# In the selective scan, VectorE runs both channel tiles' scans of a unit before the column copies and the products with C

## The reference, cut to what matters

```
xs = silu(conv(in_proj(x)))                          # 512 channels
dt = softplus(dt_proj(x_dbl[..., :16]) + dt_proj_b)
Bv, C = x_dbl[..., 16:32], x_dbl[..., 32:48]         # 16 states
a = exp(dt[..., None] * A)                           # A = -exp(A_log)
u = dt[..., None] * Bv[:, :, None, :] * xs[..., None]
h[t] = a[t] * h[t-1] + u[t]                          # along time, for each channel and state
y = einsum('btis,bts->bti', h, C) + xs * D_skip
```

## Time and profile before

| what | value |
|---|---|
| median of the runs | 2456.8 us (2453.07 to 2459.64) |
| the profiled execution, first to last instruction | 2453.7 us |
| PE busy | 2211.1 us (90%) |
| DVE busy | 1888.8 us (77%) |
| ACT busy | 1647.0 us (67%) |
| POOL busy | 1373.5 us (56%) |
| DMA | 430.22 MB, mean 175 GB/s |
| granted TensorE clock, mean | 0.957 |

### The profile page before, as it was taken

The page is one execution under the profiler, slowest core; times in us unless marked ns, Lnnn a source line. Parts: engine busy times, 40 slices in busy tenths (PEclk is TensorE's granted clock), DMA queues, the critical chain, the costliest instruction groups (busy, mean ns, idle before and its releaser), DMA issues.

```text
span 2453.7 us, 36941 instructions
## 1 busy us (share of the span) xinstructions
PE 2211.1 (90%) x12464; PEld 1794.1 (73%) x12464; DVE 1888.8 (77%) x3049; ACT 1647.0 (67%) x2715; POOL 1373.5 (56%) x809
## 2 busy tenths in 40 slices
PE   6788887999999996998799999999999999899986
PEld 4778776798888895887566767666676676676765
DVE  5686654566666662676898998989989899899995
ACT  6755542455555552666778787887788877878774
POOL 0103333011111115221888988989889988899895
PEclk8899988999999997999799999999999999999988
DMA  8434334566666653533465656655556566565562
GB/s 285 83 50 102 89 95 125 189 230 230 230 229 231 230 209 103 177 112 115 159 212 183 195 172 198 210 183 186 189 175 216 181 193 201 184 202 169 186 206 99
DMA packets 235434, 430.22 MB, mean 175 GB/s; under 512 B 35089, under 2 KB 117457, under 8 KB 235234
## 3 DMA queue, kind: packets, MB, share of 16 engines
q1 hardware_dynamic: 229090, 410.87, 52.3%
q0 software_dynamic: 6144, 16.79, 2.2%
HBM read 353.61 MB, written 73.96 MB: 174 GB/s over the span
## 4 chain that ended last, share of the span: by engine, by line
PE 51%; DVE 16%; issue 12%; ACT 9%; POOL 5%; DMA 4%; SPq 1%; another core or an unknown queue 1%; POOLq 1%; DVEq 0%; ACTq 0%
PE pb L1643 11%; PE pb L1616 11%; DVE pb L2096 6%; PE pb L2408 4%; PE pb L2413 4%; PE pb L996 3%; PE pb L2434 2%; PE pb L2307 2%; DVE UU L2102 2%; POOL UU L2021 2%; PE pb L2323 2%; DMA XB<-xnd 2%; PE pb L2332 2%; POOL UU L2029 1%; ACT L2233 1%
## 5 line engine op out<-in xcount | busy, mean ns | idle before, releaser
L2021 POOL TENSOR_TENSOR UU<-dx,BB 128x1024 f32<-128x1024 f32 x256 | 616.5, 2417 | 108.5 <-DMA BB<-bcd 83.7
L2233 ACT ACTIVATE pb<-dt,al 128x512 f32<-128x512 f32 x512 | 339.5, 686 | 147.9 <-DVE UU L2102 146.5
L2102 DVE TENSOR_TENSOR UU<-pb,CC 128x512 f32<-128x512 f32 x512 | 351.4, 686 | 22.4 <-DMA CC<-bcd 4.8
L2096 DVE TENSOR_TENSOR_SCAN pb<-pb,hs,UU 128x512 f32<-128x512 f32 x256 | 328.5, 1283 | 12.2 <-ACT pb L2233 8.0
L2096 DVE TENSOR_TENSOR_SCAN pb<-pb,UU 128x512 f32<-128x512 f32 x256 | 312.9, 1222 | 7.8 <-ACT pb L2233 6.4
L1533 DVE TENSOR_TENSOR HL<-HF,HH 128x512 fp32r<-128x512 f32 x220 | 159.7, 728 | 206.6 <-ACT HH L1438 198.9
L1433 ACT ACTIVATE HF<-pb,BU 128x512 f32<-128x512 f32 x192 | 132.1, 688 | 245.9 <-PE pb L1616 195.9
L1383 POOL TENSOR_TENSOR clo_b<-craw_b,chi_b 128x1024 fp32r<-128x1024 f32 x22 | 62.3, 2830 | 409.9 <-ACT chi_b L1446 409.9
L2408 PE MATMUL pb<-HAh,WH 128*128 128x512 f32 x1024 | 279.3, 415 | 8.2 <-DVE dt L2077 6.3
L1643 PE MATMUL pb<-W2h,HH 128*128 128x256 f32 x880 | 256.6, 292 | 6.3 <-issue 5.0
L2413 PE MATMUL pb<-HAl,WH 128*128 128x512 f32 x1024 | 258.2, 394 | 0.0
(11 more groups left out here) (333 smaller groups left out, 4880.3 us busy)
## 6 DMA issues: line engine op xcount, KB each, us to landing
WH<-fhd SPq DMA_DIRECT2D x176, 512.0 KB, 3.5
BB<-bcd SPq DMA_DIRECT2D x256, 256.0 KB, 4.7
CC<-bcd SPq DMA_DIRECT2D x256, 256.0 KB, 5.0
raw<-in_w1a SPq DMA_DIRECT2D x23, 1024.0 KB, 7.2
raw<-in_w2a SPq DMA_DIRECT2D x23, 1024.0 KB, 7.7
craw_b<-in_fch SPq DMA_DIRECT2D x22, 512.0 KB, 6.3
fhd<-chi_b SPq DMA_DIRECT2D x22, 512.0 KB, 3.9
fld<-clo_b SPq DMA_DIRECT2D x22, 512.0 KB, 5.1
```

The costliest lines, as they stand in the source:

```text
L2021: e.tensor_tensor(ubuf(n)[:], dx[p][:], BB[n % 3][:].rearrange("p (a m) -> p a m", a=1).to_broadcast([P, 2, 512]), ALU.mult).then_inc(p_u. ...
L2096: e.tensor_tensor_scan(h_[:], h_[:], uu[:, c, :], first, ALU.mult, ALU.add).then_inc(v_sc.sem, 1)
L2102: e.tensor_tensor(uu[:, c, :], abank(n, c)[:], CC[n % 3][:], ALU.mult).then_inc(v_mu.sem, 1)
L2233: e.activation(abank(n, c)[:], dt[p][:, c, :], ACT.Exp, scale=al1[:, 2 * p + c, s:s + 1]).then_inc(c_a.sem, 1)
```

## The change

In step `u` of VectorE's loop, the order of a unit was scan 0, copy 0, product 0, scan 1, copy 1, product 1. It becomes scan 0, scan 1, copy 0, product 0, copy 1, product 1. Copies exist in even blocks only. The wait for `CC` moves from behind scan 0 to behind scan 1. The waits for the finished scan of each tile (`v_sc`) stay in front of its copy and product. The number of instructions and their tiles are unchanged, as are the counts that the other engines wait for: `v_sc` still counts tile 0 before tile 1, and so do `c_hs` and `v_mu`.

```diff
@@ -2094,11 +2094,11 @@
                         else:
                             first = 0.0
                         e.tensor_tensor_scan(h_[:], h_[:], uu[:, c, :], first, ALU.mult, ALU.add).then_inc(v_sc.sem, 1)
-                        if c == 0:
-                            e.wait_ge(s_cl[n % 3], 16 * (n // 3 + 1))
+                    e.wait_ge(s_cl[n % 3], 16 * (n // 3 + 1))
+                    for c in range(2):
                         e.wait_ge(*v_sc.at((p, s, c), blk))
                         if blk % 2 == 0:
-                            e.tensor_copy(hs[:, 2 * i + c:2 * i + c + 1], h_[:, 511:512]).then_inc(c_hs.sem, 1)
+                            e.tensor_copy(hs[:, 2 * i + c:2 * i + c + 1], abank(n, c)[:, 511:512]).then_inc(c_hs.sem, 1)
                         e.tensor_tensor(uu[:, c, :], abank(n, c)[:], CC[n % 3][:], ALU.mult).then_inc(v_mu.sem, 1)
```

## The result

The changed kernel took 2486.3 us, the median of four runs (2484.6 to 2487.9), against 2455.5 us before: a ratio of 1.0123, interval 1.0108 to 1.0138. It is 31 us slower, more than the forecast of 2460 us and beyond the range, which ended at 2482 us. In a second comparison, beside other runs of both kernels, the ratio was 1.0113 (1.0088 to 1.0138). The profiled execution spans 2482.6 us.

The account below looks back on a forecast made before the run. The prediction saw no single engine as the bound, but a chain hopping between engines in strict order, with PE the floor. Its terms, -19 + 15 + 8 + 0 = +4 us, gave 2460 us, range 2434 to 2482.

Parts of the forecast that it names:

- Step 1: DVE's scans back to back: a unit falls from 3.92 to about 3.6 us, worth -19 us for scans on the path.
- rival (c): On DVE, a scan behind a scan does not overlap, so only the costs remain: 2480 us, chance 0.06.
- Step 2: Tile 0's product comes 0.97 us later; 15 handovers through ACT to PE, at units 14 and 25, cost +15 us.
- Step 3: ACT's other work W behind the waiting exponential stops DVE above 2.8 us, before 4.4; longer stops cost +8 us.
- Step 4: DVE's wait for CC moves behind scan 1; most of its 13.7 us disappears, counted as 0 us.
- (b): Tile 0's bank decides, where ACT's exponential waits with a table load behind it: +19 us, 2476 us, chance 0.30.
- unit pace: Sign on DVE: a unit without stops takes 3.6 us instead of 3.92.
- ACT's wait above 146.5 us: Sign on ACT: its wait for products to free a bank stays near or above 146.5 us.
- its mark of 50 us: Sign on DVE: idle time before scans with ACT as releaser rises from 14.5 us to 50 or more.

Follow-up runs that it names:

- the four-bank pair: Kernel before and changed kernel, each with four PSUM banks for the scans instead of three: 0.9984 and 0.9968 against the kernel before.
- the twelve units: Kernel before with the new order only in 12 units a block where tile 1's exponential started 0.9 us or more after product 0: 1.0001.
- the 17 units: Kernel before with the new order in the 12 units a block where no exponential waits, and in 6, 16, 17, 20 and 24: 0.9969.
- The units with long W: Kernel before with the new order in 13 units a block, nearly all with 3.9 us or more of ACT's work behind the waiting exponential: 1.0090.
- six places: Kernel before with the new order in units 6, 14, 16, 17, 20 and 24, with 1.7 us or less of ACT's work behind the exponential: 0.9960.
- four of 32: Changed kernel with the old order in units 25, 27, 29 and 31 of each block: 0.9995 against the kernel before.

## Why the prediction was wrong, step by step

**Step 1, DVE's pace**, was right in its size and wrong in its worth. Scan behind scan runs at 1.13 us (two in 2.35 us, the copy 2.26 us behind the first at 1646.99 in the trace of after), and a unit takes 3.6 us. But the term of -19 us for scans on the path was a wrong use of the chain. The chain's share says where the last result passed, and not that the rest would keep up. With the handovers gone, in the four-bank pair, the gain was some 5 us; in the twelve units there was none.

The rule of the Trainium skill's "VectorE: DVE Perf Modes", section "The DRAIN you can't avoid", that led to rival (c) does not hold here in its plain form. A scan that depends on nothing before it starts 1.13 us after one that lasts 1.2. The same section adds that a next operation that is not held starts earlier, and this the trace bears out.

**Step 2, the handover at units 14 and 25**, forecast +15 us from ACT's work that leads to PE. The lateness per handover was right: product 0 starts 2.31 us after scan 0 in an even block (1635.47 to 1637.78), 0.91 us later than before. With the new order in unit 25 alone PE's wait for silu rose by 6.6 us, near the 7 x 0.97 of the forecast. In the changed kernel the two waits that were to rise by 15 us rose by 2.2: for XB from 8.2 to 8.7 us and for silu from 12.5 to 14.2. Adding unit 14 to the 17 units cost nothing that can be told apart. So the term was too high, and it hid what was missing in step 3.

**Step 3, the slack between ACT and DVE**, is the step that failed. It had the loop, the place and the point from which it decides (W above 2.8 us), and then counted the 24 old stops alone, made each 0.97 us longer, and put a third of these 23 us on the path, +8. The new stops were named and given no price. In the runs DVE's stops for exponentials grew by 61 us (16.5 to 78), in 82 stops instead of 29. The units with long W cost 0.90%, 22 us, and unit 25 with 6.4 us behind it 0.63%, 15 us, of which XBl's collision may hold a part. With a fourth bank the loss was gone. The step also priced only the wait for the exponential, and not that for softplus, which ACT does in the same order (13.7 to 26.8 us, with PE's wait behind it from 6.3 to 15.2).

**Step 4, CC**: the waits went from 13.7 us to 3.2 (1.8 before the copies and 1.4 before the products), and it was worth nothing, as said.

**What was not in it**: XBl's collision with POOL. The late product 0 of unit 25 shifted XBh by about a microsecond, and that turned around which of the two waits for the other. Its share is open, since no run removes it and keeps the late handover of unit 25. It takes 2.05 us of DVE's time in each of seven blocks, 14 us. The kernel with the old order in unit 25 bounds it together with that handover: 1.0074 against 1.0113 or 1.0123. And 0.74% is lost without it, so it is not the main cause.

The forecast gives itself two slightly different bands, 2452 to 2466 and 2449 to 2464 us; the result lies outside both. Of the rivals, (b) named the mechanism that won, at 2476 us and with a chance of 0.30. It was too cheap for the same reason as step 3. What the forecast said would show it did: unit pace, CC, ACT's wait above 146.5 us. DVE's wait for exponentials passed its mark of 50 us as well: 39.8 us by the profile's name, and 66 us with the 26.1 us that it calls issue. So the waits came as foreseen, and it was their price that was wrong.

## What to carry to other kernels

Where two engines hand buffers back and forth, price a reordering by when each buffer is released and by the work queued behind whoever waits for it, and not by the busy time saved. Divide the places by the length of that queued work before you change them all: here six places gained 0.4%, thirteen lost 0.9%, and four of 32 cost as much as the whole net loss. When an experiment shortens an instruction to take a collision away, read in its trace whether the wait went too. A chain's share for an engine is no gain that a faster engine would bring when three engines stand within a few per cent of each other.

## What the runs showed of the hardware

When VectorE's subtraction with both inputs in SBUF and GpSimd's multiply overlap, one of them is stretched by the other's time, and which one depends on 0.2 us. In the eight blocks, XBl lasted 1.21 to 1.22 us seven times before, starting at most 0.26 us ahead of the multiply, which then took 3.2 to 3.4 us. It lasted 3.25 to 3.39 us seven times after, starting 0.04 to 0.17 us behind the multiply, which kept its 2.35; GpSimd's next addition then took 3.33 to 3.34. Cut to 16 columns, XBl still took 2.21 to 2.35 us behind the multiply, and 0.16 to 0.17 us where it did not start behind one. The Trainium skill's "SBUF — State Buffer", section "SBUF: two separate sides", states this: the shared port pair is an exclusive lock, and whichever starts first has it for the whole instruction. The trace agrees, 3.27 us against 1.22. Scans and products, which read one input from PSUM, kept their 1.2 and 0.68 us beside the same multiplies.

What stays open: how much XBl's collision costs in the changed kernel, how the place of a unit and its W share the loss, and what holds ACT's exponentials back in the new order with four banks, where DVE's saved time turns into waits for them.
